# Attention over pixels: from one image in bf16 parts to two images at once in fp32

## The reference

```python
def _prelu(x, a):
    return jnp.where(x >= 0, x, a * x)
e1 = _conv1x1(x, w1, b1, a1)     # 64 -> 32 channels, prelu
e2 = _conv1x1(x, w2, b2, a2)     # 64 -> 32 channels, prelu
asm = _conv1x1(x, wa, ba, aa)    # 64 -> 64 channels, prelu
score = softmax(einsum('nci,ncj->nij', e1, e2), axis=2)   # 2304 x 2304 per image
out = einsum('nij,ncj->nci', score, asm)
x = x + out
```

## Time and profile before

| | us |
|---|---|
| median of 3 runs (2034.74 to 2035.96) | 2035.14 |
| the profiled execution | 2033.85 |
| its span | 2032.1 |
| TensorE busy | 1496.4 (74%) |
| VectorE busy | 1458.9 (72%) |
| ScalarE busy | 918.7 (45%) |
| GpSimd busy | 741.8 (37%) |

### The profile page before, as it was taken

One profiled execution on the slowest core, in us unless ns is written; L12 is line 12 of the kernel. 1 busy time (PEld: TensorE's weight loads), 2 busy tenths in 40 slices (PEclk: granted clock), 3 DMA queues, 4 the chain that ended last, 5 costly groups with the idle time before them and its releaser, 6 DMA issues. The chain is left out here.

```text
span 2032.1 us, 29658 instructions
## 1 busy us (share of the span) xinstructions
PE 1496.4 (74%) x7816; PEld 642.1 (32%) x7816; DVE 1458.9 (72%) x2365; ACT 918.7 (45%) x1454; POOL 741.8 (37%) x637
## 2 busy tenths in 40 slices
PE   0894008885075999999999995444799897997957
PEld 0552005452032333333333333221233232332323
DVE  2346988996138899999999994465698696984542
ACT  2555043321135777777777772240154343443530
POOL 1001318996023233223233230200266474665810
PEclk9997559998576899999999997665599898998978
DMA  3000000000120000000000000033000000000023
GB/s 72 0 0 0 0 0 1 0 0 1 38 45 20 20 20 19 19 19 19 19 19 24 25 10 1 0 70 70 1 0 1 1 0 1 0 0 1 0 99 59
DMA packets 30237, 35.43 MB, mean 17 GB/s; under 512 B 19648, under 2 KB 21956, under 8 KB 29684
## 3 DMA queue, kind: packets, MB, share of 16 engines
q1 hardware_dynamic: 30177, 34.69, 7.0%
HBM read 21.60 MB, written 5.35 MB: 13 GB/s over the span
## 5 line engine op out<-in xcount | busy, mean ns | idle before, releaser
L1214 ACT ACTIVATE xp_sb<-ps 120x768 f32<-120x768 f32 x432 | 351.1, 813 | 142.4 <-PE ps L1163 86.9
L1569 POOL TENSOR_TENSOR arena_sb<-arena_sb 128x384 f32<-128x384 f32 x288 | 301.7, 1047 | 236.5 <-ACT arena_sb L1693 126.5
L1273 POOL TENSOR_SCALAR arena_sb<-arena_sb 120x1152 f32<-120x1152 f32 (+2 forms) x168 | 172.5, 1027 | 416.0 <-DVE arena_sb L1246 416.0
L1246 DVE SCALAR_TENSOR_TENSOR arena_sb<-xp_sb 120x384 f32<-120x384 f32 x432 | 310.8, 719 | 17.2
L1693 ACT ACTIVATE arena_sb<-ps 128x384 f32<-128x384 f32 x432 | 200.2, 489 | 264.3 <-PE ps L1619 240.7
L1710 DVE TENSOR_REDUCE arena_sb<-ps 128x1 f32<-128x384 f32 x432 | 215.6, 550 | 84.5 <-PE ps L1605 82.5
L1163 PE MATMUL ps<-arena_sb 109*120 (+1 forms) x864 | 234.0, 358 | 7.0 <-ACT xp_sb L1214 4.7
L1239 DVE TENSOR_SCALAR xp_sb<-xp_sb 120x384 f32<-120x384 f32 x432 | 195.0, 451 | 36.0 <-ACT xp_sb L1214 32.3
L1184 PE MATMUL ps<-arena_sb 120*64 120x216 f32 x1536 | 184.7, 363 | 32.8 <-POOL arena_sb L1273 17.0
L1627 PE MATMUL ps<-arena_sb 128*64 128x384 f32 x864 | 190.5, 522 | 0.0
L1195 PE MATMUL ps<-xp_sb,arena_sb 64*64 64x384 f32 x864 | 184.5, 506 | 6.9 <-ACT xp_sb L1225 6.9
(11 more groups left out here) (222 smaller groups left out, 1961.1 us busy)
## 6 DMA issues: line engine op xcount, KB each, us to landing
arena_sb<-pixel_major SPq DMA_DIRECT2D x96, 120.0 KB, 2.2
arena_sb<-xp_sb SPq DMA_DIRECT2D x40, 144.0 KB, 3.1
arena_sb<-in_W SPq DMA_DIRECT2D x1, 4608.0 KB, 13.7
pixel_major<-arena_sb SPq DMA_DIRECT2D x24, 108.0 KB
x_sb<-in_x SPq DMA_DIRECT2D x4, 576.0 KB, 8.6
out_x<-x_sb SPq DMA_DIRECT2D x24, 96.0 KB, 2.2
arena_sb<-arena_sb SPq DMA_DIRECT2D x8, 144.0 KB, 3.4
arena_sb<-in_sel SPq DMA_DIRECT2D x1, 919.7 KB
```

The costliest lines, as they stand in the source:

```text
L1214: act.activation(mag[s % 2], p_d[s % 2], ACT.Abs).then_inc(S["abs"], 1)
L1246: v_.scalar_tensor_tensor(bmat[par][:, CH * s:CH * s + CH], mag[s % 2][:, 0, :], 1.0, mag[s % 2][:, 1, :], ALU.subtract, ALU.mult).then_in ...
L1273: pool.tensor_scalar(part, part, 1.0, 0.0, ALU.min, ALU.max).then_inc(S["b"], 1)
L1569: eng.tensor_tensor(acc, a, pt[j % SLOTS], ALU.add).then_inc(S[name], 1)
```

## The change

Layer 2 is written anew; the other layers stay as they are.

The projection takes all four images by one matmul group: queries of the four images come to lie in q4 and keys in k4, 32 partitions each, in fp32. The prelu is made from two Relu evictions on ScalarE and one combination on VectorE. There are no bf16 parts. Eight DMAs lay copies with a free row 32 in each half of the partitions (qp, kp); nothing waits for them before the first score. POOL writes ones in row 32 of kp, and the zeroing of xp is moved here from attend2.

In attend2 the maxima are computed for the four images at once: four matmuls of 32 rows each, into four PSUM banks, and one reduction of all four. The maxima of a chunk of all images are turned and laid by four DMAs as row 32 of qp, so that a score is one fp32 matmul of 33 rows. Two images (h = 0, 1) are done at once: scores in two tiles of 64 rows, one exponential of 128x768, values in two tiles of 64 columns. A block is one chunk of two images; there are 12, of 9 periods with two key tiles each. 21 steps of maxima (LEAD) come ahead of the first period, the others one per period. The maxima, the sums and the turned maxima share PSUM banks, and the maxima and the scores have one buffer each. POOL adds 14 of 18 tiles and VectorE 4, VectorE merges both, and one pair of matmuls sums them. ScalarE copies the output and the sums out of PSUM, and VectorE finishes both images with one reciprocal, one product and one addition of 128 partitions. All loops are written out.

In `load_stage` the weights of e1 and e2 are laid out by kind, and `neg` (5 columns) holds negated biases and slopes. The removed code is that printed above; the added, cut to its core:

```diff
+         ("e_ps", "e_split", "e_out", "v_ps", "v_biased", "v_split", "v_out", "ones", "steps")}
+    buf = [work[:, CH * i:CH * i + CH] for i in range(14)]
+    up, down = (buf[0:2], buf[2:4]), (buf[4:6], buf[6:8])
+    ya, up_v, down_v = buf[8:10], buf[10:12], buf[12:14]
+    p_e = [[ps[:, 512 * (2 * par + e):512 * (2 * par + e) + CH] for e in range(2)] for par in range(2)]
+    p_v = [ps[:, 512 * (4 + par):512 * (4 + par) + CH] for par in range(2)]
+    four = (q4, k4)
+
+    def chunks():
+        for n in range(2 * CPI):
+            yield n, n % 2, CH * n, slice(TPC * n, TPC * n + TPC)
...
+            pool.memset(ones, 1.0).then_inc(S["ones"], 1)
...
+            for i in range(CPI):
+                if i >= 2:
+                    pe.wait_ge(S["e_split"], 2 * (i - 1))
+                for e in range(2):
+                    for b2 in range(2):
+                        mm = pe.matmul(p_e[i % 2][e][64 * b2:64 * b2 + 64, :], k["l2w"][:, 64 * e:64 * e + 64],
+                                       xn[:, PIX * b2 + CH * i:PIX * b2 + CH * i + CH], start=True, stop=True)
+                    mm.then_inc(S["e_ps"], 1)
+            for n, par, at_col, _ in chunks():
+                if n >= 2:
+                    pe.wait_ge(S["v_biased"], n - 1)
+                    mm = pe.matmul(p_v[par][:, PT * t:PT * t + PT], xn[:, at_col + PT * t:at_col + PT * t + PT],
+                mm.then_inc(S["v_ps"], 1)
...
+            act.wait_ge(S["steps"], 2)
+            for i in range(CPI):
+                for e in range(2):
+                    act.wait_ge(S["e_ps"], 2 * i + e + 1)
+                    if i >= 2:
+                        act.wait_ge(S["e_out"], 2 * i + e - 3)
...
+            v.tensor_scalar(neg[:, 0:2], k["l2b"][:, :], -1.0, None, ALU.mult).then_inc(S["steps"], 1)
+            v.tensor_scalar(neg[:, 2:5], al[:, :], -1.0, None, ALU.mult).then_inc(S["steps"], 1)
+            v.wait_ge(S["steps"], 2)
+            for i in range(CPI):
+                for e in range(2):
+                    v.wait_ge(S["e_split"], 2 * i + e + 1)
+                    v.scalar_tensor_tensor(four[e][:, CH * i:CH * i + CH], down[i % 2][e], neg[:, 2 + e:3 + e],
...
+            def biased(n, par):
+                v.wait_ge(S["v_ps"], n + 1)
+                if n >= 2:
+                    v.wait_ge(S["v_split"], n - 1)
+                v.tensor_tensor(ya[par].rearrange("p (t c) -> p t c", c=C), p_v[par].rearrange("p (t c) -> p t c", c=C),
+                    .then_inc(S["v_biased"], 1)
...
+            sp.wait_ge(S["e_out"], 2 * CPI)
+            for u in range(NB):
+                b2, h = divmod(u, 2)
+                for src, dst in ((k4, kp), (q4, qp)):
+                    sp.dma_start(dst[64 * h:64 * h + HID, PIX * b2:PIX * b2 + PIX], src[HID * u:HID * u + HID, :])\
+                        .then_inc(loaded, 16)
+
+
+def attend2(nc, k, at, q4, k4, qp, kp, ones, loaded, work):
+
+    ps, x = k["psum"], k["x"]
+    W2 = 2 * CH
+    pt = [work[:, W2 * i:W2 * i + W2] for i in range(SLOTS)]
+    o = W2 * SLOTS
+    acc_pool = [work[:, o + W2 * i:o + W2 * i + W2] for i in range(2)]
+    acc_v = work[:, o + 2 * W2:o + 3 * W2]
+    both = work[:, o + 3 * W2:o + 4 * W2]
+    o += 4 * W2
...
+    BLOCKS = 2 * CPI
+    PERIODS = BLOCKS * NP
+    NM = 3 * CPI
+    MAXIMA = CPI * NM
+    LEAD = NM + 3
+    TURN, SUM = NP + 6, 3
+
+    V_TILES = [4, 5, 10, 11]
+    P_TILES = [j for j in range(NJ) if j not in V_TILES]
+    V_ADDS, P_ADDS = len(V_TILES) - 1, len(P_TILES) - 1
+
...
+    def adds_after(tiles, blk, j):
+
+        return blk * (len(tiles) - 1) + max(1, tiles.index(j))
+
+    def turning(p):
+
+        ib, kk = divmod(p, 2 * NP)
+        return kk == TURN and ib + 1 < CPI
+
+    def summing(p):
+
+        return p >= NP and p % NP == SUM
+
+    def maximum(p):
+
+        return LEAD + p if LEAD + p < MAXIMA else None
...
+        @block.sync
+        def _(sp):
+            for ib in range(CPI):
+                sp.wait_ge(S["row"], ib + 1)
+                for u in range(NB):
+                    b2, h = divmod(u, 2)
+                    sp.dma_start(qp[64 * h + HID:64 * h + HID + 1, PIX * b2 + CH * ib:PIX * b2 + CH * ib + CH],
+                                 mrow[3 * u:3 * u + 3, :]).then_inc(S["row_set"], 16)
+
+        @block.tensor
+        def _(pe):
+            def maxima(m):
+                ib, r = divmod(m, NM)
+                a, jc = divmod(r, CPI)
+                if m:
+                    pe.wait_ge(S["reduced"], m)
+                for u in range(NB):
+                    own = slice(HID * u, HID * u + HID)
+                    mm = pe.matmul(p_m[:, u, :], q4[own, CH * ib + PT * a:CH * ib + PT * a + PT],
+                                   k4[own, CH * jc:CH * jc + CH], start=True, stop=True)
+                mm.then_inc(S["pairs"], 1)
+
+            def turn(ib, issued):
+                pe.wait_ge(S["maxima"], ib + 1)
+                pe.wait_ge(S["reduced"], issued)
+                pe.transpose(p_turn, mx, k["ident"][:, :]).then_inc(S["turned"], 1)
+
+            def sums(blk, issued):
+                pe.wait_ge(S["merged"], blk + 1)
+                pe.wait_ge(S["reduced"], issued)
+                for h in range(2):
+                    mm = pe.matmul(p_sum[64 * h:64 * h + 64, :], ones, acc_v[:, CH * h:CH * h + CH],
+                                   start=True, stop=True)
+                mm.then_inc(S["sums"], 1)
+
+            def scores(g):
+                ib, r = divmod(g, 2 * NJ)
+                b2, j = divmod(r, NJ)
+                if r == 0:
+                    pe.wait_ge(S["row_set"], 16 * NB * (ib + 1))
+                if g:
+                    pe.wait_ge(S["probs"], g)
+                for h in range(2):
+                    own = slice(64 * h, 64 * h + HID + 1)
+                    key = PIX * b2 + PT * j
+                    mm = pe.matmul(p_s[:, h, :], kp[own, key:key + PT],
+                                   qp[own, PIX * b2 + CH * ib:PIX * b2 + CH * ib + CH], start=True, stop=True)
+                mm.then_inc(S["scores"], 1)
+
+            def values(g):
+                blk, j = divmod(g, NJ)
+                b2 = blk % 2
+                pe.wait_ge(S["probs"], g + 1)
+                if j == 0 and blk:
+                    pe.wait_ge(S["both_out"], blk)
+                for h in range(2):
+                    mm = pe.matmul(p_o[64 * h:64 * h + 64, :], at[:, b2 * TPI + j, 64 * h:64 * h + 64],
+                                   pt[g % SLOTS][:, CH * h:CH * h + CH], start=(j == 0), stop=(j == NJ - 1))
+                mm.then_inc(S["values"], 1)
+
+            for m in range(NM):
+                maxima(m)
+            turn(0, NM)
+            pe.wait_ge(S["row"], 1)
+            for m in range(NM, LEAD):
+                maxima(m)
+            pe.wait_ge(loaded, 16 * 2 * NB)
+            for p in range(PERIODS):
+                new = p and p % NP == 0
+                issued = min(LEAD + p, MAXIMA)
+                m = maximum(p)
+                scores(2 * p)
+                if new:
+                    values(2 * p - 1)
+                if turning(p):
+                    turn(p // (2 * NP) + 1, issued)
+                elif summing(p):
+                    sums(p // NP - 1, issued)
+                elif m is not None:
+                    maxima(m)
+                scores(2 * p + 1)
+                if p and not new:
+                    values(2 * p - 1)
+                if (turning(p) or summing(p)) and m is not None:
+                    if summing(p):
+                        pe.wait_ge(S["sums_out"], p // NP)
+                    else:
+                        pe.wait_ge(S["row"], p // (2 * NP) + 2)
+                    maxima(m)
+                values(2 * p)
+            values(2 * PERIODS - 1)
+            sums(BLOCKS - 1, MAXIMA)
+
+        @block.scalar
+        def _(act):
+            def probs(g):
+                act.wait_ge(S["scores"], g + 1)
+                if g >= SLOTS:
+                    blk, j = divmod(g - SLOTS, NJ)
+                    act.wait_ge(S["values"], g - SLOTS + 1)
+                    if j in V_TILES:
+                        act.wait_ge(S["v_added"], adds_after(V_TILES, blk, j))
+                    else:
+                        act.wait_ge(S["pool_added"], adds_after(P_TILES, blk, j))
+                act.activation(pt[g % SLOTS].rearrange("p (h n) -> p h n", h=2), p_s, ACT.Exp)\
+                    .then_inc(S["probs"], 1)
+
+            def keep(blk):
+                act.wait_ge(S["values"], NJ * (blk + 1))
+                if blk:
+                    act.wait_ge(S["added"], blk)
+                act.activation(both[:, 0:CH], p_o, ACT.Copy).then_inc(S["both_out"], 1)
+
+            def keep_sums(blk):
+                act.wait_ge(S["sums"], blk + 1)
+                if blk:
+                    act.wait_ge(S["added"], blk)
+                act.activation(total, p_sum, ACT.Copy).then_inc(S["sums_out"], 1)
+
+            for p in range(PERIODS):
```

(113 more changed lines are left out.)

311 lines of the change are left out of this document (46 added, 265 removed), and 2 rows, old and new, of the table k.

## The result

After the change the kernel takes 2075.62 us (median of 4 runs, 2074.11 to 2078.12) against 2035.01 (2034.74 to 2035.96) for the kernel before on the same chip: a ratio of 1.020 (1.0182 to 1.0218). It is 40.6 us slower. The forecast was 2004, its range ended at 2060. The profiled execution stands at 2075.64.

What follows compares the result with a forecast made beforehand. TensorE was taken to bound the blocks, chains of waits the first two stretches; 33 + 1 + 73.7 + 5 + 487 + 9 = 608.7 us against 640 gave span 2001, forecast 2004 us, range 1955 to 2060.

Steps and rivals of the forecast that it cites:

- The projection: Start of the changed stage: 12 steps on both image pairs and 12 value steps, 33 us in place of 93.
- The lead-in: Maxima ahead of the blocks: 18 steps of 3.45 us, 1.2, and three more steps; 73.7 us in place of 60.8.
- The period: Blocks: two key tiles of two images in 4.11 us, with a maximum or without; 108 periods, 444 us.
- Maxima that don't run abreast: Rival: a maximum group holds TensorE 1.47 us instead of 0.80, giving 2066 us; chance 0.10.
- a shorter chain: Rival: periods at TensorE's own 3.84 us with the finish hidden, giving 1955 us; chance 0.15.
- contended exponentials: Rival: contended exponentials or costlier changes of tile shape make a period 4.4 us, giving 2035 us, no change; chance 0.10.
- The block with its sum and half a turn: Per block: in periods of the sums and the turn the maximum leaves the gap, costing 0.96 us each; 12.5 us altogether.
- The stall: TensorE's maximum waits for VectorE's reduction, delayed by finishing work: 3.3 us in each of 9 blocks, 30 us.
- the steady sum: All steady periods: 444 + 12.5 + 30 = 487 us, with 5 more for the first two at 1.2 GHz.
- the clock falls in the VectorE stall: Rival: two periods behind each stall run at 1.2 GHz, 5 us in each of 9 blocks, giving 2049 us; chance 0.12.
- two slow periods: First two periods of the blocks run at 1.2 GHz, adding 5 us.
- The row that was held against the rival: Projection before, 1320.4 to 1323.8: TensorE busy 1.08 of 3.4 us at clock 1.00, cited against the clock falling in stalls.

Runs made afterwards that it cites:

- the spread finish: Kernel after with VectorE's reciprocal ahead of its period's reduction, product behind it, addition to x a period later: 2012.41 us, ratio 0.9886 to before.
- filled lead-in: Kernel after plus two unread fp32 matmul pairs behind each of 21 early maxima: 2061.21 us; the 36.6 us block also had VectorE's finish reordered and last periods filled.
- filler and spread finish: Kernel after with VectorE's finish reordered and one unread fp32 matmul pair in 18 of the last 21 periods: 1980.51 us, ratio 0.9734 to before.
- filled end: Kernel after plus one unread fp32 matmul pair in 18 of the last 21 periods, which have no maximum: 2059.34 us, ratio 1.0149 to before.
- all three: Kernel after with VectorE's finish reordered and unread fp32 matmuls in both the last periods and the lead-in: 1957.69 us, ratio 0.9619 to before.

## Why the prediction was wrong

By its own steps:

- The projection was put at 33 us and took 29. Right, 4 us better.
- The lead-in was put at 73.7 us and took 73.3, at the clock of 0.50 assumed, in steps of 3.54 (forecast 3.45). Right.
- The period was put at 4.11 and took 4.11 to 4.12 while the clock was 1.00, with the maximum in the gap behind one score buffer. Right. Maxima that don't run abreast, a shorter chain and contended exponentials, three of the rivals, are excluded by the same rows.
- The block with its sum and half a turn, without stall, comes to 38.4 in the forecast (9 x 4.11 + 0.96 x 1.5) and to 39.25 in the kernel with the spread finish. Some 0.8 us too low, 7 us over 9 blocks.
- The stall was put at 3.3 us in 9 blocks, 30 us. It is there, at the place and behind the instructions named, 9 times (3.80 as an idle row, 3.5 net in a block). The addition to x took 2.04 us beside POOL, where the forecast had 1.0.
- The failed step is the one that carried the steady sum: that all 108 periods but two run at 2.4 GHz. The forecast looked at exactly this and gave it 0.12, as the rival "the clock falls in the VectorE stall", priced at 5 us a block. It happened, in every one of the 9 blocks: 3.9 us as the mean of blocks 2 to 9 and 2.7 in block 10, 34 us.
- The first block is part of the same step. The forecast added 5 us for two slow periods; the clock came back only at about 1428, and the block takes 46.0 us where it takes 36.6 behind a filled lead-in. That is some 5 us more than the 5 put down.
- Not seen at all was the last stretch. The forecast took a period to be 4.11 "with a maximum or without", which is true of the chain and not of the clock. Blocks 11 and 12 took 101.9 us in the kernel after and 71.7 with filler and spread finish: 30 us more, of which the wait of 2.51 in place of 0.91 is 1.6. The kernel with the spread finish alone, which has neither stall, took 104.7 for them. This is why the rival's own figure, 2049, was too low and the upper end of the range, 2060, too.

The miss of 71.6 us is then 34 for the clock behind the stalls, 30 for the last two blocks, 5 for the first, 7 for the block and 2 for the stall, less 5 for the projection (29 in place of 33 + 1) and some 1 for lead-in and tail: 72. That the last stretch is the clock is shown by its rows at 0.50 and by the kernels with a filled end.

The row that was held against the rival, 1.08 us busy of 3.4 at a clock of 1.00, was one window of a few microseconds and showed nothing of what comes after it; less than 5 us later the clock was down. The kernel before also had waits like the stall, between its images, and the clock fell at each of the three. The trace of before, two stretches and then TensorE:

```profile
1328.20:1334.90 6.70, 4.57 (x14) 3.21 (x14) 5.10 (x13) 2.97 (x6) 0.74 (x1) 0.50 0.00 0
...
1578.00:1590.00 12.00, 5.79 (x17) 1.59 (x18) 2.20 (x9) 2.45 (x5) 3.18 (x4) 0.50 0.01 1
```

```profile
1584.36 0.50 PE L1618 MATMUL ps<-arena_sb 99*128 99x384 bf16 x1 [3.68 <-DMA arena_sb<-arena_sb]
```

That wait of 3.68 follows one of 5.96, so it doesn't price one wait alone, but it speaks for the rival and the forecast didn't use it. The rows that it did use for the rival were busy 50 of 62 us and still at 0.50. The same came back in the last stretch, 54.5 of 60. The Trainium skill, TensorE: Matmul & The Clock Gate, Loop structure matters more than you think, says that a long wait in front of every matmul makes TensorE go cold. The trace agrees for the waits of 3.80 us in the blocks; the waits of 0.91 in the kernel with the spread finish alone are no long ones, and for them the measurement stands by itself. With that rule the forecast would have been 2049, nearer than 2004.

The Trainium skill, TensorE: Matmul & The Clock Gate, Part 3, has a gain of 3.07 and not 4 for four row tiles, which would have made the maximum longer than a score of two tiles. Here both took alike: 0.93 and 0.92 us at 2.4 GHz, 1.66 and 1.65 at 1.2.

## What to carry to other kernels

When a change makes TensorE wait at a fixed place of each block, price the wait twice: once as time, once as the work behind it at 1.2 GHz; here the second was the larger (3.9 us against 3.5). Look in the trace of before for waits of that length and read the clock behind them. Ask the same of stretches where an interleaved part of TensorE's work ends before the rest: with less work to do, a period came to take 6.9 us instead of 4.1. The cures were cheap: move other engines' finishing work so that no wait is long, and where a gap can't be closed, put matmuls into it that nobody reads.

## What the runs showed of the hardware

- With the spread finish alone the clock fell to 1.2 GHz among periods of 4.1 us whose waits were 0.91 us at most, at about 1803, 1817 and 1827; in the kernel after the same periods had kept 1.00 from 1860 to 1890. Once down it stayed down for more than 60 us though TensorE was busy for 54.5 of 60. With one pair of fp32 matmuls in the gap (and the finish spread) it held 1.00 until 1880, for the last 85 us of it without maxima.
- Where the clock was mended in part only, the runs of one kernel lie further apart: 14 to 24 us from lowest to highest in five kernels, against 4 in the kernel after, 6 with the spread finish and filled end, 4 with all three. In each the shortest run has the highest granted clock and the longest the lowest (0.873 to 0.861 with the spread finish alone). What decides it from run to run isn't shown.
- The addition of 128x384 to x took 2.04 us in the kernel after, beside a POOL addition that began 0.39 us before it and took 2.02. With the spread finish the same addition took 0.55 (at 1513.71), and it was two POOL additions around it that took 4.60 together. Undisturbed the same addition takes 0.56 (at 1982.30) and a POOL addition 1.80. So beside each other the one or the other took longer, and which one differed.
- Four fp32 matmuls in tiles of 32 rows took no longer than two in tiles of 64 rows: 0.93 and 0.92 us.
